# A Mamba scan on one core: the first convolution tap on GpSimd, the second batch's preparation two chunks sooner

## The chip, the core and the metric

The kernel runs on one core of a Trainium2 chip. The core has engines with a queue of instructions each: TensorE (PE: matmuls and transposes), VectorE (DVE), ScalarE (ACT), GpSimd (POOL) and SyncE (SP), which here only issues DMAs. A queue runs in the order in which it is written, and engines wait for one another on semaphores. The metric is the device time of one execution in microseconds (us); lower is better.

## The reference, cut to what matters

The reference takes x of shape (2, 1024, 128) through six layers: FFN, attention, FFN, mixture of experts (MoE), Mamba, MoE. Each stands behind a layer norm and is added back to x. The change lies in the Mamba layer, in float32, and where the MoE before it ends:

```python
x = x + 0.5 * _L1_ffn_ref(_layernorm(x, axis=-1), ...)        # MoE; "combining" adds its rows to x
x = x + _L1_attn_ref(_layernorm(x, axis=-1), ...)             # Mamba, forward and backward
# in one direction of Mamba:
zxbcdt = u @ Wi.T                                             # z, x|B|C (512 channels), dt
conv = conv_general_dilated(pad(xBC_t), conv_w, ...)          # 4 taps for each channel, along time
xBC = silu(conv + conv_b)
dt = softplus(dt + dt_bias);  A = -exp(A_log)                 # "step sizes"
h = h * exp(dt_t * A) + (dt_t * x_t) * B_t;  y_t = h @ C_t    # scan over 1024 steps
y = (y + D * x) * silu(z);  y = y * rsqrt(mean(y * y) + 1e-5) * norm_w;  out = y @ Wo.T
```

## The kernel before, in words

`moe_mamba_moe` (from L2363) writes the queues of all engines out by hand, for MoE, scan and MoE. The scan has four units, each one direction of one batch (units 0 and 1 are batch 0, units 2 and 3 are batch 1). A unit is worked off in 8 chunks of 128 time steps; `u` is the unit, `i` the chunk in it, and `g = 8 * u + i` counts chunks through. I write "chunk 1.2" for unit 1, i = 2. While unit u is scanned, the input of unit u + 1 is prepared, and these tables say in which chunk:

```python
PIECES_AT = [(0,), (1,), (2,), (3,), (), (4,), (5,), ()]
TAPS_AT = [((0, 1), (0, 2)), ((0, 3), (1, 1)), ((1, 2), (1, 3)), ((2, 1), (2, 2)), ((2, 3), (3, 1)), ((3, 2), (3, 3)), (), ()]
```

A unit's input has six pieces of 128 channels: pieces 0 to 3 are x|B|C and go through the convolution, 4 and 5 are z. PE projects a piece in two halves (L2083) into two PSUM banks that are used in turn, each taken again only when its last reader is through. ACT copies a half out to `mb_padded` (L2097), and then multiplies the whole row by the first tap into `mb_act` (L2110, `first_tap`). DVE adds taps 1 to 3 (L2119, `convolve`): the pair (c, k) in TAPS_AT is piece c, tap k. A tap 1 waits for the first tap of its piece. In chunk i = 6 ACT loads the Silu table, puts piece 4 and the four convolved pieces through Silu (L2097, L2126), and only then can PE transpose the next unit's first chunk.

In each chunk DVE does, in this order: `front(g + 1)` (`mb_xdt` L2184 and `mb_gm` L2188 from PSUM, then `mb_mt` L2191 from `mb_e_seg`, which ACT makes with an Exp, L2166), `pass_state(g)` (`mb_h` L2237 or L2234), `back(g)` (`mb_y_old` L2270, `mb_y_in` L2272 or L2274), the output additions of the unit before, the taps of TAPS_AT, and what else is put into the chunk. POOL does `mb_xw` of g + 1 (L2203), the gate of g (`mb_z`, L2281) and the decayed state for g + 1 (`mb_h_dec`, L2222). ACT's `exps(g + 1)` (L2159, L2164, L2166) needs `mb_cums`, which SP loads by a DMA, and PE's transposed B (L2145).

Batch 1's preparation is spread over these chunks: `combine` (L1823, L1825) and `stats_of` (L1110, L1116) add the MoE's rows to x and take means and variances; ACT takes the root (`norm.root`, a Sqrt table, L1121); DVE normalises (`norm.normalise`, L1150, L1156); PE transposes (`norm.turn`, L1164) and ACT copies out (`norm.copy`, L1171). Then PE's `steps` (L1940) gives the raw step sizes, DVE's `step_sizes` (part 0 at L2051 and L2053, parts 1 to 3 from L2056 to L2070) and ACT's `exp_dt` (L1963) turn them into dt and decays, and PE's `sums` with ACT's `exp_sums` into their running sums.

## Time and profile before

| | |
|---|---|
| median of 3 runs | 825.32 us (821.44 to 828.21) |
| the profiled execution, its own time | 819.01 us |
| its span in the trace | 817.2 us |
| scan (from the first `mb_xdt` to the last chunk) | about 471 to 673 us in the trace |
| busy share of the span | PE 88%, DVE 60%, ACT 66%, POOL 34% |

Times in rows are microseconds from the start of the span. The shares are means over stages that have different limits, so the stretch from 471 to 673 us has to be read by itself. A row of the timeline gives the start, the busy time, the engine, the line, the operation with output and inputs, and in square brackets how long the engine was idle before it and what ended that. Several equal instructions in sequence stand as one row with their count.

### The profile page before, as it was taken

Reading aid. Unit: us, or ns where it says so; the run is one execution under the profiler, and the core shown is the slowest. Engines: PE = TensorE matmul, PEld = TensorE weight load, DVE = VectorE, ACT = ScalarE, POOL = GpSimd, SP = SyncE. Lnnn points to the kernel's source line nnn. Section 1 sums busy time; section 2 is a strip of 40 time slices with the busy share of each in tenths; the row PEclk is TensorE's granted clock in tenths of the full one; section 3 lists DMA queues with packets and bytes.
Section 4 is the critical chain, followed back from the end, with each engine's and each line's share of the span. In section 5 each row is a group of like instructions: output and inputs, shape, how many; then the busy total and the mean of one; then the engine's idle time right before and its main releaser. Section 6 shows DMA issues by size and latency. Waiting matters only on the chain. (4 is left out here: it accounts for less than half of the span.)

```text
span 817.2 us, 13088 instructions
## 1 busy us (share of the span) xinstructions
PE 715.5 (88%) x4076; PEld 377.9 (46%) x4076; DVE 489.4 (60%) x1424; ACT 542.0 (66%) x934; POOL 275.2 (34%) x296
## 2 busy tenths in 40 slices
PE   4799999979999997988988867798888987999996
PEld 1432222212223223555655545576575775566564
DVE  6878442204766565763466649789697875533453
ACT  5367998888998993653357666885987642434441
POOL 3090003301000342435522445343443380265552
PEclk9899999999999997999999988899998898999999
DMA  4056934521493311112121031121211231222233
GB/s 136 1 203 165 186 86 88 207 76 53 138 317 85 110 37 40 44 34 62 42 80 46 26 109 60 52 65 53 74 60 50 81 84 39 65 61 57 67 99 92
DMA packets 76409, 70.10 MB, mean 86 GB/s; under 512 B 9687, under 2 KB 60233, under 8 KB 76080
## 3 DMA queue, kind: packets, MB, share of 16 engines
q1 hardware_dynamic: 71024, 60.56, 26.6%
q0 software_dynamic: 5024, 8.54, 3.2%
q8 instruction: 36, 0.59, 0.3%
q14 instruction: 37, 0.30, 0.1%
q10 hardware_dynamic: 288, 0.10, 0.0%
HBM read 41.23 MB, written 29.02 MB: 86 GB/s over the span
## 5 line engine op out<-in xcount | busy, mean ns | idle before, releaser
L693 ACT ACTIVATE attn_p<-attn_ps 128x1024 f32<-128x1024 f32 x256 | 241.1, 1083 | 28.5 <-PE attn_ps L686 17.2
L709 PE MATMUL attn_ps<-attn_p,attn_v 128*32 128x512 f32 x1024 | 138.1, 611 | 5.5 <-issue 5.5
L1687 PE MATMUL ps_main<-moe_xsT,moe_w 128*128 128x320 f32 x384 | 127.9, 459 | 8.5 <-DVE moe_hid L1712 3.3
L1697 ACT ACTIVATE moe_act_h<-ps_main 128x320 f32<-128x320 f32 (+1 forms) x128 | 55.2, 434 | 102.5 <-PE ps_main L1687 72.2
L1712 DVE TENSOR_TENSOR moe_hid<-moe_act_h,ps_main 128x320 f32<-128x320 f32 (+1 forms) x128 | 61.9, 485 | 91.1 <-ACT moe_act_h L1697 57.4
L1580 POOL DMA_INDIRECT moe_slots<-rows,moe_scatter_at x64 | 63.4, 991 | 103.0 <-DVE moe_hid L1712 53.8
L1687 PEld LDWEIGHTS ps_main<-moe_xsT,moe_w 128*128 128x128 f32 x384 | 68.8, 195 | 42.5 <-issue 21.8
L686 PE MATMUL attn_ps<-attn_q_rows,attn_k_rows 64*128 64x512 bf16 x448 | 80.6, 388 | 6.4 <-issue 3.1
L1717 PE MATMUL ps_main<-moe_hid,moe_w 128*128 128x320 f32 (+1 forms) x256 | 73.3, 451 | 4.6 <-DVE moe_hid L1712 4.6
L686 PEld LDWEIGHTS attn_ps<-attn_q_rows,attn_k_rows 64*128 64x128 bf16 x448 | 19.1, 93 | 124.0 <-ACT attn_p L693 99.0
L2119 DVE SCALAR_TENSOR_TENSOR mb_act<-mb_padded,mb_taps,mb_act 128x1024 f32<-128x1024 f32 x48 | 65.9, 1382 | 9.0 <-ACT mb_act L2110 8.3
L1717 PEld LDWEIGHTS ps_main<-moe_hid,moe_w 128*128 128x128 f32 (+1 forms) x256 | 41.1, 188 | 33.0 <-issue 13.1
L2281 POOL TENSOR_TENSOR mb_z<-mb_y_in,mb_z 128x256 f32<-128x256 f32 x24 | 26.4, 1098 | 49.8 <-DVE mb_y_in L2272 32.4
L1798 POOL DMA_INDIRECT moe_rows<-moe_y,moe_dest x33 | 31.9, 966 | 32.3 <-ACT moe_y L1789 13.6
L709 PEld LDWEIGHTS attn_ps<-attn_p,attn_v 128*32 128x32 f32 x1024 | 20.5, 108 | 47.1 <-issue 35.3
L1201 POOL TENSOR_TENSOR x_sb<-x_sb,bout_half 128x1024 f32<-128x1024 f32 (+1 forms) x4 | 7.3, 1822 | 103.5 <-DVE rows L1156 103.5
L2159 ACT ACTIVATE mb_e_seg<-mb_cums,mb_cum_col 128x128 f32<-128x128 f32 x128 | 40.5, 390 | 1.7 <-DMA mb_cums<-mb_cum_kept 1.7
L442 POOL TENSOR_SCALAR attn_parts<-attn_q 128x512 bf16<-128x512 f32 x4 | 2.5, 617 | 110.0 <-DVE attn_q L398 110.0
L2191 DVE TENSOR_TENSOR mb_mt<-mb_e_seg,mb_gm 128x512 f32<-128x512 f32 x32 | 26.4, 825 | 18.3 <-ACT mb_e_seg L2166 15.9
L2203 POOL TENSOR_TENSOR mb_xw<-mb_xdt,mb_to_end 128x256 f32<-128x256 f32 x28 | 18.5, 662 | 54.0 <-DVE mb_xdt L2184 54.0
L2083 PE MATMUL ps_side<-norm_xT,mb_w_xbc 128*128 128x512 f32 x64 | 31.8, 618 | 0.0
L727 DVE COPY attn_mixed<-attn_ps 128x512 f32<-128x512 f32 x10 | 6.9, 687 | 41.6 <-PE attn_ps L709 41.6
(268 smaller groups left out, 1304.5 us busy)
## 6 DMA issues: line engine op xcount, KB each, us to landing
mb_cums<-mb_cum_kept SPq DMA_DIRECT2D x32, 256.0 KB, 3.4
moe_slots<-zeros SPq DMA_DIRECT2D x4, 1380.0 KB, 13.4
attn_q_rows<-attn_q_parts SPq DMA_DIRECT2D x36, 128.0 KB
attn_k_rows<-attn_k_parts SPq DMA_DIRECT2D x36, 128.0 KB
moe_w<-in_w SPq DMA_DIRECT2D x3, 1536.0 KB, 11.6
moe_rows<-zeros SPq DMA_DIRECT2D x4, 1024.0 KB, 14.7
moe_back<-moe_rows SPq DMA_DIRECT2D x16, 256.0 KB, 3.8
mb_e_cum<-mb_e_cum_kept SPq DMA_DIRECT2D x56, 64.0 KB, 2.7
```

Of the source, the lines that this page charges most:

```text
L686: ins = self.core.nc.tensor.matmul(into, self.k_rows[rows, ring, pair, keys], self.q_rows[rows, ring, pair, queries], start=True, stop=True)
L693: self.core.nc.scalar.activation(self.p[:, w % self.PB, :, :].rearrange("p a n -> p (a n)"), self.ps_s[:, w % self.SB, :, :].rearrange("p ...
L709: ins = self.core.nc.tensor.matmul(self.ps_av[32 * i:32 * i + 32, :], self.v[:, b * TPB + kt, (HGROUPS * i + m) // 2, self.window(m)], sel ...
L1580: nc.gpsimd.indirect_dma_start(self.slots[r], bass.IndirectOffsetOnAxis(self.scatter_at[:, b, k, j:j + 1], 0), self.row_of[:, b * TPB + j, ...
L1687: self.core.nc.tensor.matmul(ps[:, w % 2, 0:CAP], wt[:, e, c * P:(c + 1) * P], self.xsT[:, u % 2, :], start=True, stop=True).then_inc(self ...
L1697: self.core.nc.scalar.activation(self.act_h[into, w % 2, :], self.ps_h1[rows, w % 2, 0:CAP], ACT.Silu).then_inc(self.silu_done, 1)
L1712: self.core.nc.vector.tensor_tensor(self.hid[rows, u % 2, c, :], self.act_h[rows, w % 2, :], bank[rows, w % 2, 0:CAP], ALU.mult)\
L1717: return self.core.nc.tensor.matmul(self.y_bank(u)[:, 0:CAP], self.w2[rows, u % E_, c, :], self.hid[rows, u % 2, c, :], start=start, stop= ...
L1798: self.core.nc.gpsimd.indirect_dma_start(self.rows[u // E_], bass.IndirectOffsetOnAxis(self.dest[0:n, u % self.DEST, s:s + 1], 0), self.y[ ...
L2083: self.core.nc.tensor.matmul(bank[:], weight, self.xT[:, t0:t0 + BANK], start=True, stop=True).then_inc(self.proj_done, 1)
L2119: ins = self.core.nc.vector.scalar_tensor_tensor(out, src, tap, out, ALU.mult, ALU.add)
L2159: ins = nc.scalar.activation(self.e_seg[:, g % 2, hh, :], self.cums[:, g % 2, hh, :], ACT.Relu, bias=self.cum[:, di, n, hh:hh + 1], scale= ...
```

## The change: what it does

- First taps move from ACT to POOL: `first_tap_beside` is a `tensor_scalar` of 128x1024 with (tap, 1.0). The first tap of piece 0 stands ahead of the gate in chunk i = 0; those of pieces 1, 2 and 3 stand at the end of POOL's chunks i = 1, 2, 3.
- Piece 0 of units 1, 2 and 3 is projected and copied out one chunk sooner: before the first chunk for unit 1, in chunk 0.7 for unit 2 and in chunk 1.7 for unit 3.
- Batch 1's combining and statistics move from chunks 0.3 and 0.4 to 0.1 and 0.2; roots from 0.6 to 0.4; normalising from 0.6 to 0.4; PE's turns from 0.7 to 0.5, and their copies with them.
- `steps` moves from chunk 1.1 to 0.7, `step_sizes` part 0 from 1.1 to 0.7, parts 1 to 3 from 1.2 to 1.0, `exp_dt` from 1.2 to 0.7, `sums` from 1.3 to 1.1 and `exp_sums` from 1.4 to 1.1.

On POOL, chunks 0.0 and 0.1, before (`mb_xw` L2203, the gate `mb_z` L2281, `mb_h_dec` L2222):

```order
L2203 TENSOR_TENSOR mb_xw<-mb_xdt,mb_to_end 128x256 x2
L2281 TENSOR_TENSOR mb_z<-mb_y_in,mb_z 128x2x128
L2222 TENSOR_TENSOR mb_h_dec<-mb_h,mb_whole 128x256
L2203 TENSOR_TENSOR mb_xw<-mb_xdt,mb_to_end 128x256
L2281 TENSOR_TENSOR mb_z<-mb_y_in,mb_z 128x2x128
L2222 TENSOR_TENSOR mb_h_dec<-mb_h,mb_whole 128x256
```

and with the change (the same lines stand seven further down):

```order
L2210 TENSOR_TENSOR mb_xw<-mb_xdt,mb_to_end 128x256 x2
L2117 TENSOR_SCALAR mb_act<-mb_padded,mb_taps 128x1024
L2288 TENSOR_TENSOR mb_z<-mb_y_in,mb_z 128x2x128
L2229 TENSOR_TENSOR mb_h_dec<-mb_h,mb_whole 128x256
L2210 TENSOR_TENSOR mb_xw<-mb_xdt,mb_to_end 128x256
L2288 TENSOR_TENSOR mb_z<-mb_y_in,mb_z 128x2x128
L2229 TENSOR_TENSOR mb_h_dec<-mb_h,mb_whole 128x256
L2117 TENSOR_SCALAR mb_act<-mb_padded,mb_taps 128x1024
```

The first tap of piece 1 (the second L2117) stands behind the gate and `mb_h_dec` of its chunk; the one of piece 0 stands ahead of the gate.

On DVE, from the taps of chunk 0.4 to the taps of chunk 0.5, with the change (before, L1823 to L1116 stood where L1150 and L1156 stand here, and the two pairs of L1150 and L1156 stood in chunk 0.6, behind the last taps):

```order
L2126 SCALAR_TENSOR_TENSOR mb_act<-mb_padded,mb_taps,mb_act 128x1024 x2
L1150 RECIPROCAL norm_rstd<-norm_std 128x4
L1156 TENSOR_SCALAR rows<-x_sb,norm_mv,norm_rstd 128x128 x4
L1150 RECIPROCAL norm_rstd<-norm_std 128x4
L1156 TENSOR_SCALAR rows<-x_sb,norm_mv,norm_rstd 128x128 x4
L2191 TENSOR_TENSOR mb_xdt<-ps_main,mb_dt 128x256
L2195 TENSOR_TENSOR mb_gm<-ps_main,mb_incl 128x128
L2198 TENSOR_TENSOR mb_mt<-mb_e_seg,mb_gm 128x512
L2244 TENSOR_TENSOR mb_h<-mb_h_dec,ps_main 128x256
L2277 TENSOR_TENSOR mb_y_old<-mb_e_cum,ps_main 128x256
L2279 TENSOR_TENSOR mb_y_in<-mb_y_old,ps_main 128x256
L2126 SCALAR_TENSOR_TENSOR mb_act<-mb_padded,mb_taps,mb_act 128x1024 x2
```

Normalising batch 1 now lies between the taps of two chunks, ahead of `mb_xdt` of chunk 0.6.

On ACT, from the four Silus of chunk 0.6 to the Exp for chunk 1.1, before:

```order
L2126 ACTIVATE mb_act<-mb_act,mb_conv_b 128x1024 x4
L2097 ACTIVATE mb_z<-ps_side 128x512 x2
L2290 ACTIVATE mb_y<-mb_z 128x256
L2159 ACTIVATE mb_e_seg<-mb_cums,mb_cum_col 128x128 x4
L2164 COPY mb_bs<-ps_main 128x128
L2166 ACT_TABLE_LOAD
L2166 ACTIVATE mb_e_seg<-mb_e_seg 128x512
L2290 ACTIVATE mb_y<-mb_z 128x256
L1171 COPY norm_xT<-ps_side 128x512 x2
L2159 ACTIVATE mb_e_seg<-mb_cums,mb_cum_col 128x128 x4
L2164 COPY mb_bs<-ps_main 128x128
L2166 ACTIVATE mb_e_seg<-mb_e_seg 128x512
```

and with the change:

```order
L2133 ACTIVATE mb_act<-mb_act,mb_conv_b 128x1024 x4
L2097 ACTIVATE mb_z<-ps_side 128x512 x2
L2297 ACTIVATE mb_y<-mb_z 128x256
L2166 ACTIVATE mb_e_seg<-mb_cums,mb_cum_col 128x128 x4
L2171 COPY mb_bs<-ps_main 128x128
L2173 ACT_TABLE_LOAD
L2173 ACTIVATE mb_e_seg<-mb_e_seg 128x512
L2297 ACTIVATE mb_y<-mb_z 128x256
L2097 ACTIVATE mb_padded<-ps_side 128x512 x2
L1963 ACTIVATE mb_ex<-mb_ab 128x64
L2166 ACTIVATE mb_e_seg<-mb_cums,mb_cum_col 128x128 x4
L2171 COPY mb_bs<-ps_main 128x128
L2173 ACTIVATE mb_e_seg<-mb_e_seg 128x512
```

The two copies of the normalised rows have left, and the two halves of piece 0 of unit 2 and the Exp of the step sizes (L1963) now stand ahead of `mb_e_seg` for chunk 1.1.

The diff:

```diff
--- before.py
+++ after.py
@@ -2109,6 +2109,13 @@
             act.wait_ge(self.y_read, self.NC * (u - 1))
         self.core.nc.scalar.activation(self.act_t[:, u % 2, c, :], src, ACT.Copy, scale=tap).then_inc(self.tapped, 1)
 
+    def first_tap_beside(self, pool, u, c):
+        src, tap = self.window(u, c, 0)
+        pool.wait_ge(self.proj_read, (u * self.PIECES + c) * 2 + 2)
+        if u >= 2:
+            pool.wait_ge(self.y_read, self.NC * (u - 1))
+        self.core.nc.gpsimd.tensor_scalar(self.act_t[:, u % 2, c, :], src, tap, 1.0, ALU.mult, ALU.mult).then_inc(self.tapped, 1)
+
     def convolve(self, dve, ch, u, c, k):
 
         (src, tap), out = self.window(u, c, k), self.act_t[:, u % 2, c, :]
@@ -2449,6 +2456,7 @@
                 pe.wait_ge(moe.y_read, 3 * HALF)
                 pe.wait_ge(mamba.norm_done, 2)
                 mamba.before(pe, 0)
+                mamba.project(pe, 1, 0)
                 for g in range(N):
                     u, i = g // NC, g % NC
                     if g + 1 < N:
@@ -2464,15 +2472,19 @@
                         mamba.output(pe, u, i - 6)
                     if u == 1 and i == 0:
                         pe.wait_ge(norm.ready, 20)
+                    if u == 0 and i == 5:
+                        norm.turn(pe, 18)
+                        norm.turn(pe, 19)
                     if u + 1 < UNITS:
                         for c in mamba.PIECES_AT[i]:
-                            mamba.project(pe, u + 1, c)
+                            if c:
+                                mamba.project(pe, u + 1, c)
+                    if u + 2 < UNITS and i == 7:
+                        mamba.project(pe, u + 2, 0)
                     if u == 0 and i == 7:
-                        norm.turn(pe, 18)
-                        norm.turn(pe, 19)
+                        pe.wait_ge(norm.ready, 20)
+                        mamba.steps(pe, 1)
                     if u == 1 and i == 1:
-                        mamba.steps(pe, 1)
-                    if u == 1 and i == 3:
                         mamba.sums(pe, 1)
                     if u == 2 and i == 7:
                         norm.turn(pe, 20)
@@ -2578,10 +2590,14 @@
                     u, i = g // NC, g % NC
                     if g + 1 < N:
                         mamba.to_state(pool, g + 1)
+                    if u < 3 and i == 0:
+                        mamba.first_tap_beside(pool, u + 1, 0)
                     if u < 3:
                         mamba.gate(pool, nc.gpsimd, g)
                     if i < NC - 1:
                         mamba.decay(pool, g + 1)
+                    if u < 3 and i in (1, 2, 3):
+                        mamba.first_tap_beside(pool, u + 1, i)
                     if u == 3 and 2 <= i <= 6:
                         moe.scatter(pool, 3, 3 * (i - 2), 3 * (i - 1) + (i == 6))
                 for u in range(HALF, 2 * HALF):
@@ -2674,15 +2690,15 @@
                     if u + 1 < UNITS:
                         for c, k in mamba.TAPS_AT[i]:
                             mamba.convolve(dve, ch, u + 1, c, k)
-                    if u == 0 and i in (3, 4):
-                        moe.combine(dve, ch, 1, i - 3)
-                        norm.stats_of(dve, ch, i + 15)
-                    if u == 0 and i == 6:
+                    if u == 0 and i in (1, 2):
+                        moe.combine(dve, ch, 1, i - 1)
+                        norm.stats_of(dve, ch, i + 17)
+                    if u == 0 and i == 4:
                         norm.normalise(dve, ch, 18)
                         norm.normalise(dve, ch, 19)
-                    if u == 1 and i == 1:
+                    if u == 0 and i == 7:
                         mamba.step_sizes(dve, ch, 1, 0)
-                    if u == 1 and i == 2:
+                    if u == 1 and i == 0:
                         for part in range(1, mamba.STEP_PARTS):
                             mamba.step_sizes(dve, ch, 1, part)
                     if u == 2 and i == 4:
@@ -2781,13 +2797,14 @@
                 moe.weigh(act, HALF - 1)
                 mamba.take(act, 0, 5)
                 mamba.exps(act, 0)
+                mamba.take(act, 1, 0)
                 for g in range(N):
                     u, i = g // NC, g % NC
                     if g + 1 < N:
                         mamba.exps(act, g + 1)
                     if g == 1:
                         act.wait_ge(moe.y_out[(HALF - 2) % moe.OUT], moe.landings(HALF - 2))
-                    if u == 0 and i == mamba.GATES_AT:
+                    if u == 0 and i == 4:
                         norm.root(act, 18)
                         norm.root(act, 19)
                     if u == 2 and i == mamba.GATES_AT:
@@ -2802,20 +2819,21 @@
                         mamba.deviation(act, 3)
                     if u + 1 < UNITS:
                         for c in mamba.PIECES_AT[i]:
-                            if c < 4:
+                            if 1 <= c < 4:
                                 mamba.take(act, u + 1, c)
-                                mamba.first_tap(act, u + 1, c)
                         if gates:
                             mamba.take(act, u + 1, 4)
                             mamba.silu_rows(act, u + 1)
                             mamba.take(act, u + 1, 5)
                             mamba.square(act, g - 1)
-                    if u == 0 and i == 7:
+                    if u == 0 and i == 5:
                         norm.copy(act, nc.scalar.copy, 18)
                         norm.copy(act, nc.scalar.copy, 19)
-                    if u == 1 and i == 2:
+                    if u + 2 < UNITS and i == 7:
+                        mamba.take(act, u + 2, 0)
+                    if u == 0 and i == 7:
                         mamba.exp_dt(act, 1)
-                    if u == 1 and i == 4:
+                    if u == 1 and i == 1:
                         mamba.exp_sums(act, 1)
                     if u == 2 and i == 7:
                         norm.copy(act, nc.scalar.copy, 20)
```

## Rows read from the trace of the kernel before

**Rows 1.** Busy time by stretch (header first): one inside unit 0, one inside unit 1.

```profile
core 0: us, PE busy (x) PEld busy (x) DVE busy (x) ACT busy (x) POOL busy (x), PEclk, DMA share, GB/s
...
487.00:521.00 34.00, 24.50 (x148) 17.94 (x149) 32.87 (x61) 21.94 (x51) 19.12 (x15) 0.90 0.20 64
...
537.00:575.00 38.00, 34.21 (x228) 26.00 (x225) 36.51 (x74) 27.21 (x65) 15.41 (x15) 0.96 0.19 55
```

**Rows 2.** DVE timeline: first taps 1 and 2 of units 1, 2, 3.

```profile
483.84 2.61 DVE L2119 SCALAR_TENSOR_TENSOR mb_act<-mb_padded,mb_taps,mb_act 128x1024 f32<-128x1024 f32 x2 [3.93 <-ACT mb_act L2110]
...
536.76 2.60 DVE L2119 SCALAR_TENSOR_TENSOR mb_act<-mb_padded,mb_taps,mb_act 128x1024 f32<-128x1024 f32 x2 [2.32 <-ACT mb_act L2110]
...
588.12 2.61 DVE L2119 SCALAR_TENSOR_TENSOR mb_act<-mb_padded,mb_taps,mb_act 128x1024 f32<-128x1024 f32 x2 [2.10 <-ACT mb_act L2110]
```

**Rows 3.** DVE timeline, units 0 and 1: the same operations alone and beside POOL.

```profile
476.69 0.69 DVE L2191 TENSOR_TENSOR mb_mt<-mb_e_seg,mb_gm 128x512 f32<-128x512 f32 x1 [0.63 <-ACT mb_e_seg L2166]
...
489.05 2.94 DVE L2119 SCALAR_TENSOR_TENSOR mb_act<-mb_padded,mb_taps,mb_act 128x1024 f32<-128x1024 f32 x2
...
492.63 0.95 DVE L2191 TENSOR_TENSOR mb_mt<-mb_e_seg,mb_gm 128x512 f32<-128x512 f32 x1
```

**Rows 4.** POOL timeline, chunk 0.1 and the start of 0.2.

```profile
489.21 1.70 POOL L2281 TENSOR_TENSOR mb_z<-mb_y_in,mb_z 128x256 f32<-128x256 f32 x1 [1.74 <-PE ps_main L2214]
490.88 1.59 POOL L2222 TENSOR_TENSOR mb_h_dec<-mb_h,mb_whole 128x256 f32<-128x256 f32 x1
492.43 0.61 POOL L2203 TENSOR_TENSOR mb_xw<-mb_xdt,mb_to_end 128x256 f32<-128x256 f32 x1
```

**Rows 5.** POOL timeline, attention stage: TENSOR_SCALAR with one tensor input, twice 512 columns.

```profile
52.36 1.20 POOL L450 TENSOR_SCALAR attn_parts<-attn_rest 128x512 bf16<-128x512 f32 x2
```

**Rows 6.** ACT timeline, unit 0: mb_e_seg of 0.2, the tables of 0.6, the copies of 0.7.

```profile
485.14 1.28 ACT L2159 ACTIVATE mb_e_seg<-mb_cums,mb_cum_col 128x128 f32<-128x128 f32 x4 [1.33 <-DMA mb_cums<-mb_cum_kept]
...
486.47 0.63 ACT L2166 ACTIVATE mb_e_seg<-mb_e_seg 128x512 f32<-128x512 f32 x1
...
517.04 1.28 ACT L1121 ACT_TABLE_LOAD   x1
...
518.84 1.28 ACT L2097 ACT_TABLE_LOAD   x1
...
530.13 1.07 ACT L1171 COPY norm_xT<-ps_side 128x512 f32<-128x512 f32 x2
```

**Rows 7.** DVE timeline, end of unit 0: mb_xdt of 0.6, normalising batch 1, mb_xdt of 1.0.

```profile
514.71 0.39 DVE L2184 TENSOR_TENSOR mb_xdt<-ps_main,mb_dt 128x256 f32<-128x256 f32 x1
...
522.69 0.17 DVE L1150 RECIPROCAL norm_rstd<-norm_std 128x4 f32<-128x4 f32 x1
...
524.55 1.11 DVE L1156 TENSOR_SCALAR rows<-x_sb,norm_mv,norm_rstd 128x128 f32<-128x128 f32 x4
526.56 0.42 DVE L2184 TENSOR_TENSOR mb_xdt<-ps_main,mb_dt 128x256 f32<-128x256 f32 x1 [0.91 <-PE ps_main L2142]
```

**Rows 8.** DVE timeline: mb_mt of 1.0 and 1.1, step-size part 0, mb_y_in of 2.0.

```profile
529.92 0.69 DVE L2191 TENSOR_TENSOR mb_mt<-mb_e_seg,mb_gm 128x512 f32<-128x512 f32 x1 [2.74 <-ACT mb_e_seg L2166]
...
533.08 0.69 DVE L2191 TENSOR_TENSOR mb_mt<-mb_e_seg,mb_gm 128x512 f32<-128x512 f32 x1 [1.15 <-ACT mb_e_seg L2166]
...
544.91 0.21 DVE L2051 TENSOR_TENSOR mb_v<-ps_side,mb_dt_bias 128x64 f32<-128x64 f32 x1
545.16 0.38 DVE L2053 SCALAR_TENSOR_TENSOR mb_ab<-mb_v 128x64 f32<-128x64 f32 x1
...
585.60 0.41 DVE L2274 COPY mb_y_in<-ps_main 128x256 f32<-128x256 f32 x1
```

**Rows 9.** PE timeline: one piece projected, the raw step sizes, and the turns.

```profile
529.46 1.07 PE L1164 MATMUL ps_side<-ident,rows 128*128 128x128 f32 x8
...
537.77 1.96 PE L2083 MATMUL ps_side<-norm_xT,mb_w_xbc 128*128 128x512 f32 x4
539.62 1.95 PE L1940 MATMUL ps_side<-mb_w_dt,norm_xT 128*128 128x8 f32 x16
```

## The prediction

> **What bounds the kernel now.** The change touches the scan alone, so I read the busy times of its stretches first, then each engine's timeline in it, to see what ends every wait. Inside a unit DVE is the bound: it is busy 32.87 of 34 us in chunks 0.1 to 0.5 and 36.51 of 38 us in unit 1, where ACT has 21.94 and 27.21 and POOL 19.12 and 15.41 [rows 1]. What adds time to DVE's queue there adds it to the kernel; what ACT is spared there gives nothing back. Only where units meet does DVE wait for others: 3.93, 2.32 and 2.10 us, 8.35 in all, for the first tap of piece 0 of units 1, 2 and 3 [rows 2], 0.91 us for the transposes behind ACT's Silus [rows 7], and 2.74 and 1.15 us for ACT's Exp [rows 8].
>
> The timelines of DVE and POOL have to be laid side by side, since they disturb each other. `mb_mt` takes 0.69 us alone and 0.95 us where POOL's `mb_xw` started 0.20 us before it [rows 3, 4]. A pair of taps takes 2.61 us alone and 2.94 us beside POOL [rows 2, 3]. The other way, of POOL's three operations on 256 columns `mb_xw` takes 0.61 us, but beside DVE's taps `mb_h_dec` takes 1.59 and the gate 1.70 us [rows 4]. The gate starts at 489.21, beside a tap that started at 489.05 and is 1.30 us long (half of 2.61), and ends at 490.91, some 0.55 us after that tap: it sat through the tap and then ran. The one that comes second waits for the other's whole instruction.
>
> **First tap of pieces 1: DVE waits for POOL, +6.3 us.** On POOL the tap of piece 1 stands behind the gate and `mb_h_dec` of chunk i = 1. DVE's second tap in that chunk is tap 1 of this very piece and needs it. The first tap on POOL costs 1.20 us by twice 512 columns of the same operation [rows 5]; ends are 0.61 us, what a 256-column operation takes [rows 4], and 2.4 us, twice the measured 1.20. I take 1.20, since the columns are the same and one tensor is read. From the row: the gate ends at 490.91, `mb_h_dec` would run alone now, as DVE stands still, 0.61 us, then the tap 1.20 us: 492.7. DVE's tap of 1.30 us ends at 494.05, where the pair now ends at 489.05 + 2.94 = 491.99 [rows 3]. So 2.1 us in each of three units. Behind the waiting tap on DVE's queue stands the whole next chunk, so nothing takes this up.
>
> **First taps of pieces 2 and 3: +5.0 us.** They stand at the end of POOL's chunks i = 2 and 3 and are needed a chunk later, so nobody waits for their result. But in unit 0 `mb_h_dec` ends at about 492.5, when DVE's taps are over and `mb_mt` is next [rows 3, 4]: the 1.20 us then lie before `mb_mt`, combining or the next unit's taps, all with two inputs in SBUF. A POOL operation of 0.61 us costs DVE 0.95 - 0.69 = 0.26, its length less 0.35. By that one of 1.20 costs 0.85, six times 5.0. The ends are 0.26 (1.6 in all) and the whole 1.20 (7.2). The Trainium skill, SBUF — State Buffer, "Who interferes with whom", has it that a DVE operation with two SBUF inputs and a GpSimd one that reads SBUF exclude each other for the whole instruction, and that whoever issues first has the pair; by its letter a tap costs DVE nothing or all of it. The same skill's Perfetto Trace Analysis, "Optimizing Scalar/DVE Operations", warns that work passed between these two engines may not help, which speaks against this change; the rows above agree.
>
> **First tap of piece 0 and the earlier copy.** This is the gain that the change can have, up to 8.35 us.
> - Unit 1: the taps can start at 479.9 instead of 483.84, but what follows them is `mb_mt` of chunk 0.2, and its `mb_cums` lands at 485.14, after which ACT needs till 487.10 [rows 6]. That DMA's place in SP's queue doesn't change. DVE waits there instead of ahead of the taps: gain 0.
> - Unit 3: `mb_y_in` of 2.0 ends at 586.01 and the taps start at 588.12, so 2.10 is to be had [rows 2, 8]. ACT now copies piece 0 ahead of its `mb_e_seg` for chunk 2.1, 1.07 us as for the two copies of the same width [rows 6], and POOL's tap falls beside that `mb_mt`, 0.5 us. I take -0.5, from -2.1 to +0.5.
> - Unit 2 has step sizes in its way, next.
>
> **Between units 0 and 1: +1.5 us.** The order on PE in 0.7 becomes: project piece 0 (1.96 us), `steps` (1.95 us) [rows 9], and then the transposes for 1.1, where before the 1.07 us of turns stood. `steps` takes the bank that ACT must first have copied out, behind the Exp of 1.0. With 529.46 for the start: projected 531.4, `steps` done 533.4, part 0 on DVE 0.6 us [rows 8] till 534.0, `exp_dt` on ACT till 534.3, and ACT's `exps` for 1.1, 1.96 us as from 485.14 to 487.10 [rows 6], till 536.2. `mb_mt` of 1.1 comes at 536.2 where it came at 533.08: +3.1. `mb_h` and `mb_y_in` follow, and the taps start at about 538.0, not 536.76: +1.2 although the tap wait of 2.32 is gone. Ahead of this, ACT is rid of the Sqrt table and roots in 0.6 (517.04 to 518.84, 1.8 us [rows 6]). But PE's turns now wait for DVE's normalising, which ends where `mb_xdt` of 0.6 starts, at 514.7 by the rows of before [rows 7]. The second turn takes half of 1.07, a copy on ACT half of 1.07, piece 4 in the freed banks 1.96 us behind them: 517.3; the transposes for 0.7 and ACT's last two steps of `exps` take 1.7 us more, an estimate, till 519.0, where that Exp now ends at 517.0. So ACT's way to the Silus is 2.0 us longer and 1.8 us shorter. Net about +0.3. The range of both is 0 to +3.5.
>
> **Batch 1's work.** Combining and statistics move between two chunks that are both full: 0. Normalising runs from 522.69 to 525.66 now, 3.0 us in the shadow of ACT's Silus, since DVE would wait till 526.56 anyway [rows 7]. In 0.4 it has no shadow and pushes everything behind it, ACT's Silus too, since these follow the transposes that follow DVE: **+3.0**. It would cost nothing only if ACT or PE were late in 0.5, and they aren't. `step_sizes` part 0 leaves a full chunk for the wait between units: -0.6 [rows 8]. Parts 1 to 3 go from one full chunk to another, 0. `sums` and `exp_sums` move on PE and ACT, which have room inside units [rows 1]. SP's queue is the same. Twelve first taps leave ACT: 0, where it has room.
>
> **Sum.** 6.3 + 5.0 + 0 - 0.5 + 1.5 + 3.0 - 0.6 = **+14.7 us**. On the profiled execution's own 819.0 us this is 833.7; that run lies 6.3 us under the median of 825.3. Against the median I forecast **840 us**. By the lower ends (waits for piece 1 at 1.5 each = 4.5, others 1.6, -2.1, 0, 3.0, -0.6) it is +6.4, 832; by the upper ones (waits at 3.3 = 9.9 with a 2.4 us tap, 7.2, +0.5, +3.5, +3.0, -0.6) +23.5, 849. The Trainium skill, GPSIMD Engine Reference, "Engine selection", sends elementwise work to VectorE and calls GpSimd with one input roughly line-rate; taking DVE's 1.30 us for the same columns as line-rate I would estimate a sum 0.9 us higher.
>
> **Rivals.** About 1%, 8.2 us, is the least that this kernel's measurement tells from no change.
> - *A wash.* Taps cost DVE what the short POOL operations cost, 0.26 each, and the gaps between units give back what the rows hold (2.10 at unit 3, all of the 2.32 at unit 2): 6.3 + 1.6 - 2.1 - 2.3 + 3.0 - 0.6 = +5.9, 831. For it: POOL idles half of each chunk [rows 1]. Against it: POOL's idle part lies before the gate, not behind it, and the step sizes stand in the way. Chance 0.20.
> - *Faster.* The three waits for piece 0 go for good (-8.35), the roots' 1.8 us leave the way to the Silus, and POOL's taps fit: 825.3 - 10.2 = 815. It turns on chunk i = 1: if POOL's tap of piece 1 ends before DVE's first tap of that chunk does (1.3 us behind `mb_y_in`), nobody waits. For it: 3.93 us is the longest of the waits. Against: gate and `mb_h_dec` stand ahead of it and are held up by that same DVE tap [rows 4]; normalising would have to be free too. Chance 0.08.
> - *Whole-instruction lock.* By the skill's rule above, where POOL always comes first: 7.2 instead of 5.0, and the same again for the taps of piece 0 beside `mb_mt` and for `mb_xw` queued behind a tap, 1.2 us three times: +20.5, 846. For it: POOL's queue is ready at the moment at which DVE ends its taps. Against: DVE's short PSUM operations lie between and take no harm. Chance 0.10.
> - Forecast: 0.62.
>
> The range 829 to 848 takes in the forecast with its bounds, the lock and half of the wash. Faster by over 1%: 0.08. Within 1% (817 to 833.5): the wash and a little of the forecast, 0.21. Slower: 0.71.
>
> **What would show it.** Right: in chunks 0.1, 1.1 and 2.1 a wait of about 2 us on DVE for POOL's L2117 ahead of a tap, and none in front of the first taps; the wait for `mb_e_seg` in front of `mb_mt` of 0.2 grown to over 3 us; `mb_mt` over 1.2 us long behind POOL's taps of pieces 2 and 3; L1156 ahead of `mb_xdt` of 0.6 and a wait of 3 to 4 us at the end of unit 0; `mb_mt` of 1.1 over 5 us behind that of 1.0. Wrong: POOL's L2117 under 0.8 us; no wait in i = 1; DVE idle in 0.4 to 0.6, which would make normalising free; or the step from 0.7 to 1.1 not longer than before.

## The result: slower by 1.5%, and the profile after

| | before | changed |
|---|---|---|
| median of the runs shown | 825.34 us (4 runs, 821.44 to 828.21) | 833.98 us (4 runs, 830.7 to 838.54) |
| ratio | 1 | 1.0153, 95% interval 1.0109 to 1.0197 |
| profiled execution, its span | 819.0, 817.2 us | 830.7, 828.8 us |

The forecast was 840 us, 829 to 848, slower with a chance of 0.71. Runs that the chip disturbed are left out of every ratio here, and e1 and e4 below, whose only traces came from such runs, are told without one.

The scan starts 0.3 us later than before, and its last `mb_xdt` comes 11.2 us later; the span grew by 11.6 us. So all of it is in the scan. In the tables and rows that follow, lines from L2112 on have moved by 7 (the taps are L2126, `mb_xdt` L2191, `mb_mt` L2198; the new tap is L2117). The control e9 and e12 have the numbers of before, e10 and e11 numbers 3 higher than the changed kernel's.

The table of waits of the changed kernel, VectorE from 465 to 690 us (total, times, longest), answers to the three waits for ScalarE's first tap in [rows 2]: these are gone, and three for GpSimd's stand there.

```profile
DVE mb_mt L2198 <- ACT mb_e_seg L2173: 19.5, 9, 3.2
DVE mb_xdt L2191 <- PE ps_main L2149: 13.6, 4, 7.0
DVE mb_act L2126 <- POOL mb_act L2117: 6.9, 3, 2.3
DVE mb_v L2051 <- PE ps_side L1940: 3.6, 1, 3.6
```

**Piece 0.** Rows of VectorE: the taps of unit 1 and the `mb_mt` of 0.2 behind them, and, in unit 3's preparation, the `mb_mt` of 2.1 beside GpSimd's tap of 594.05 to 595.17.

```profile
479.22 2.94 DVE L2126 SCALAR_TENSOR_TENSOR mb_act<-mb_padded,mb_taps,mb_act 128x1024 f32<-128x1024 f32 x2
...
484.92 0.69 DVE L2198 TENSOR_TENSOR mb_mt<-mb_e_seg,mb_gm 128x512 f32<-128x512 f32 x1 [2.23 <-ACT mb_e_seg L2173]
...
594.34 1.37 DVE L2198 TENSOR_TENSOR mb_mt<-mb_e_seg,mb_gm 128x512 f32<-128x512 f32 x1 [1.11 <-ACT mb_e_seg L2173]
```

**Piece 1.** Chunk 0.1 on VectorE (first fence) and GpSimd (second), timeline rows of the changed kernel: start, length, what is idle before it in brackets.

```profile
486.65 1.28 DVE L2126 SCALAR_TENSOR_TENSOR mb_act<-mb_padded,mb_taps,mb_act 128x1024 f32<-128x1024 f32 x1
490.22 1.28 DVE L2126 SCALAR_TENSOR_TENSOR mb_act<-mb_padded,mb_taps,mb_act 128x1024 f32<-128x1024 f32 x1 [2.29 <-POOL mb_act L2117]
```

```profile
486.81 1.71 POOL L2288 TENSOR_TENSOR mb_z<-mb_y_in,mb_z 128x256 f32<-128x256 f32 x1 [3.60 <-DVE mb_y_in L2279]
488.47 0.61 POOL L2229 TENSOR_TENSOR mb_h_dec<-mb_h,mb_whole 128x256 f32<-128x256 f32 x1
489.07 1.12 POOL L2117 TENSOR_SCALAR mb_act<-mb_padded,mb_taps 128x1024 f32<-128x1024 f32 x1
```

The pair of taps lasts from 486.65 to 491.50, 4.85 us, where it lasted 2.94 [rows 3]: 1.9 us. The gate is held up by VectorE's first tap, `mb_h_dec` then runs its 0.61 us alone, and the tap takes 1.12 us. Chunks 1.1 and 2.1 have the same wait of 2.29 us.

**Pieces 2 and 3.** In 0.3 GpSimd's tap starts 0.18 us ahead of `mb_mt`, which takes 1.47 us and not 0.94. In 1.3 VectorE comes first: GpSimd's tap starts beside the second tap of VectorE's pair (568.96 to 571.79) and takes 2.09 us; most of what is left of it then lies beside `mb_xdt` and `mb_gm`, which read PSUM and only one tensor in SBUF, and which take no longer for it, and `mb_mt` takes 0.89 (0.94 before). VectorE's rows first, GpSimd's second.

```profile
509.71 1.47 DVE L2198 TENSOR_TENSOR mb_mt<-mb_e_seg,mb_gm 128x512 f32<-128x512 f32 x1
...
568.96 2.83 DVE L2126 SCALAR_TENSOR_TENSOR mb_act<-mb_padded,mb_taps,mb_act 128x1024 f32<-128x1024 f32 x2
571.71 0.41 DVE L2191 TENSOR_TENSOR mb_xdt<-ps_main,mb_dt 128x256 f32<-128x256 f32 x1
...
572.42 0.89 DVE L2198 TENSOR_TENSOR mb_mt<-mb_e_seg,mb_gm 128x512 f32<-128x512 f32 x1
```

```profile
509.53 1.11 POOL L2117 TENSOR_SCALAR mb_act<-mb_padded,mb_taps 128x1024 f32<-128x1024 f32 x1
...
570.68 2.09 POOL L2117 TENSOR_SCALAR mb_act<-mb_padded,mb_taps 128x1024 f32<-128x1024 f32 x1
```

These rows give the price of standing beside one another. An operation of GpSimd and one of VectorE with two inputs in SBUF run one behind the other here: the later one ends at the end of the earlier one, plus its own length alone, less 0.15 us. `mb_mt` of 0.5 (0.69 us alone): 509.53 + 1.11 + 0.69 - 0.15 = 511.18, and it ends at 511.18. GpSimd's tap in 1.3: 571.79 + 1.12 - 0.15 = 572.76, and it ends at 572.77. `mb_mt` behind it: 572.77 + 0.69 - 0.15 = 573.31, as in the row. The 0.95 us of [rows 3] come out too, behind `mb_xw` [rows 4]: 493.04 + 0.54 = 493.58. So a tap on GpSimd costs VectorE what is left of it when VectorE wants to start, and nothing where VectorE's operation is first and done before the next such one.

**End of unit 0 and start of unit 1.** VectorE first, TensorE second. They answer to [rows 7 to 9].

```profile
515.28 1.20 DVE L1156 TENSOR_SCALAR rows<-x_sb,norm_mv,norm_rstd 128x128 f32<-128x128 f32 x4
...
517.64 0.42 DVE L2191 TENSOR_TENSOR mb_xdt<-ps_main,mb_dt 128x256 f32<-128x256 f32 x1
...
529.84 0.42 DVE L2191 TENSOR_TENSOR mb_xdt<-ps_main,mb_dt 128x256 f32<-128x256 f32 x1 [4.12 <-PE ps_main L2149]
...
533.65 0.69 DVE L2198 TENSOR_TENSOR mb_mt<-mb_e_seg,mb_gm 128x512 f32<-128x512 f32 x1 [3.18 <-ACT mb_e_seg L2173]
...
541.39 0.69 DVE L2198 TENSOR_TENSOR mb_mt<-mb_e_seg,mb_gm 128x512 f32<-128x512 f32 x1 [1.54 <-ACT mb_e_seg L2173]
...
542.66 2.94 DVE L2126 SCALAR_TENSOR_TENSOR mb_act<-mb_padded,mb_taps,mb_act 128x1024 f32<-128x1024 f32 x2
```

```profile
533.18 3.76 PE L2083 MATMUL ps_side<-norm_xT,mb_w_xbc 128*128 128x512 f32 x4
536.73 1.97 PE L1940 MATMUL ps_side<-mb_w_dt,norm_xT 128*128 128x8 f32 x16
```

Normalising now stands ahead of `mb_xdt` of 0.6 (515.09 to 517.64, 2.55 us), the stretch that it filled before is a wait of 4.12 us, and `mb_mt` of 1.1 comes 7.74 us behind that of 1.0, where it came 3.16 behind it. The projection that stands ahead of the raw step sizes takes 3.76 us for the same four matmuls that took 1.96 [rows 9]. The busy times by stretch (columns as in [rows 1]) say why: TensorE was granted 0.51 of its clock there, the lower of its two levels; a figure between 0.5 and 1 is a stretch that has both.

```profile
487.00:521.00 34.00, 27.15 (x122) 19.70 (x121) 30.80 (x63) 16.43 (x40) 18.93 (x16) 0.72 0.15 47
521.00:530.00 9.00, 6.01 (x40) 4.27 (x39) 4.70 (x9) 8.21 (x12) 3.47 (x3) 1.00 0.19 45
530.00:537.00 7.00, 7.00 (x27) 4.33 (x25) 1.91 (x5) 4.52 (x12) 1.34 (x2) 0.51 0.14 47
```

### The profile page after: what moved, and what is told of

Read it like the earlier page. It is cut to its first block and busy times, and to the rows that moved or that the text cites. A ratio compares the mean times of both kernels' runs of the same rounds, so it can differ in the third digit from the quotient of the medians.

```text
span 828.8 us, 13090 instructions
## 1 busy us (share of the span) xinstructions
PE 723.8 (87%) x4076; PEld 383.7 (46%) x4076; DVE 492.9 (59%) x1424; ACT 530.1 (64%) x923; POOL 295.4 (36%) x308
## 5 line engine op out<-in xcount | busy, mean ns | idle before, releaser
L709 PE MATMUL attn_ps<-attn_p,attn_v 128*32 128x512 f32 x1024 | 136.4, 604 | 5.7 <-issue 5.6
L1697 ACT ACTIVATE moe_act_h<-ps_main 128x320 f32<-128x320 f32 (+1 forms) x128 | 55.2, 434 | 102.9 <-PE ps_main L1687 73.1
L1580 POOL DMA_INDIRECT moe_slots<-rows,moe_scatter_at x64 | 63.8, 997 | 102.9 <-DVE moe_hid L1712 54.1
L2126 DVE SCALAR_TENSOR_TENSOR mb_act<-mb_padded,mb_taps,mb_act 128x1024 f32<-128x1024 f32 x48 | 67.1, 1403 | 7.5 <-POOL mb_act L2117 6.9
L2288 POOL TENSOR_TENSOR mb_z<-mb_y_in,mb_z 128x256 f32<-128x256 f32 x24 | 29.3, 1219 | 47.5 <-DVE mb_y_in L2279 41.7
L2198 DVE TENSOR_TENSOR mb_mt<-mb_e_seg,mb_gm 128x512 f32<-128x512 f32 x32 | 27.8, 867 | 21.9 <-ACT mb_e_seg L2173 19.5
L2221 PE MATMUL ps_main<-mb_xw,mb_bs 128*128 128x256 f32 x56 | 20.7, 455 | 16.4 <-DVE mb_h L2244 5.8
L2083 PE MATMUL ps_side<-norm_xT,mb_w_xbc 128*128 128x512 f32 x64 | 32.9, 636 | 0.0
```

What stands on the lines that cost most here:

```text
L709: ins = self.core.nc.tensor.matmul(self.ps_av[32 * i:32 * i + 32, :], self.v[:, b * TPB + kt, (HGROUPS * i + m) // 2, self.window(m)], sel ...
L1580: nc.gpsimd.indirect_dma_start(self.slots[r], bass.IndirectOffsetOnAxis(self.scatter_at[:, b, k, j:j + 1], 0), self.row_of[:, b * TPB + j, ...
L1697: self.core.nc.scalar.activation(self.act_h[into, w % 2, :], self.ps_h1[rows, w % 2, 0:CAP], ACT.Silu).then_inc(self.silu_done, 1)
L2083: self.core.nc.tensor.matmul(bank[:], weight, self.xT[:, t0:t0 + BANK], start=True, stop=True).then_inc(self.proj_done, 1)
L2126: ins = self.core.nc.vector.scalar_tensor_tensor(out, src, tap, out, ALU.mult, ALU.add)
```

## Experiments: one part taken back

The theory was the sum of terms: each part taken out of the changed kernel should give its term back. All ratios here and below are to runs of the kernel before on the same chip at the same time; here the kernel before had 828.29 us.

**e1_taps_on_act**: the first taps return to ScalarE.

```diff
-                    if u < 3 and i == 0:
-                        mamba.first_tap_beside(pool, u + 1, 0)
...
-                    if u < 3 and i in (1, 2, 3):
-                        mamba.first_tap_beside(pool, u + 1, i)
...
                                 mamba.take(act, u + 1, c)
+                            if c < 4:
+                                mamba.first_tap(act, u + 1, c)
```

> The changed kernel with all twelve first taps back on ACT (piece 0's in chunk i = 0, pieces 1 to 3 behind their copies); piece 0 still copied early, batch 1's work still early. Theory (first taps on POOL cost DVE a wait of 2.3 us in i = 1, three times, and port time in i = 2 and 3, together about 9 us against 5.9 saved nowhere): no DVE wait on a first tap of piece 1, and 834 - 9 = 825 us, level with the kernel before. Rival (the cost sits in batch 1's work, moved out of the shadow of ACT's Silus and into the step between units 0 and 1): the taps' place matters little since POOL idles anyway, and this stays at 832 to 835 us.

Measured: 837.72 us, ratio 1.0099 (1.0053 to 1.0144).

**e2_taps_ahead_of_gate**: GpSimd's taps of pieces 1 to 3 stand ahead of the gate of their chunk instead of behind the decay.

```diff
+                    if u < 3 and i in (1, 2, 3):
+                        mamba.first_tap_beside(pool, u + 1, i)
                     if u < 3:
                         mamba.gate(pool, nc.gpsimd, g)
                     if i < NC - 1:
                         mamba.decay(pool, g + 1)
-                    if u < 3 and i in (1, 2, 3):
-                        mamba.first_tap_beside(pool, u + 1, i)
```

> The changed kernel with the first taps of pieces 1, 2 and 3 put ahead of the gate in POOL's chunks i = 1, 2, 3; they stay on POOL. Theory (what costs is POOL's order: gate and mb_h_dec ahead of the tap): the three waits of 2.29 us on DVE for POOL's L2117 are gone or under 0.5 us, the port time stays or grows a little, 834 - 5 = 829 us. Rival (what costs is that two engines share a read port, wherever the tap stands): the time stays within 2 us of 834, the waits turning into longer mb_mt and longer tap pairs.

Measured: 840.17 us, ratio 1.0134 (1.0063 to 1.0205).

**e3_batch1_as_before**: batch 1's combining, normalising, turning and step sizes stand where they stood before; GpSimd keeps the taps, and pieces 0 of units 1 and 3 stay early.

```diff
-                    if u == 0 and i in (1, 2):
-                        moe.combine(dve, ch, 1, i - 1)
-                        norm.stats_of(dve, ch, i + 17)
-                    if u == 0 and i == 4:
+                    if u == 0 and i in (3, 4):
+                        moe.combine(dve, ch, 1, i - 3)
+                        norm.stats_of(dve, ch, i + 15)
+                    if u == 0 and i == 6:
                         norm.normalise(dve, ch, 18)
...
-                    if u == 0 and i == 7:
+                    if u == 1 and i == 1:
                         mamba.step_sizes(dve, ch, 1, 0)
```

> The changed kernel with all of batch 1's work (combining, roots, normalising, turns, step sizes, sums) and piece 0 of unit 2 back in their old chunks; first taps stay on POOL, piece 0 of units 1 and 3 stays early. Theory (normalising in 0.4 costs DVE 2.55 us, and the longer way from 0.7 to 1.1 costs 4.6 less the 2.3 of the tap wait): about 5 us less, 829 us; the wait ahead of mb_xdt of 1.0 is down from 4.12 to 1 us. Rival (batch 1's work only changes place between full chunks and the taps on POOL cost everything): 834, no less than 832 us.

Measured: 843.45 us, ratio 1.0183 (1.0112 to 1.0255).

**e4_steps_as_before**: only the step sizes of batch 1 (the second hunk above, with the matmuls and exponentials that belong to it) go back.

> The changed kernel with only the step sizes of batch 1 (steps, step_sizes, exp_dt, sums, exp_sums) back in chunks 1.1 to 1.4; normalising stays in 0.4 and unit 2's piece 0 stays early. Theory (steps in 0.7 stands between the transposes of 1.0 and 1.1 on PE and so holds up mb_mt of 1.1, 4.6 us later against mb_mt of 1.0 than before): mb_mt of 1.1 comes some 4 us behind mb_mt of 1.0 and not 7.7, part 0 costs 0.6 in 1.1: 834 - 3 = 831 us. Rival (the piece's projection at 1.2 GHz, 3.76 us, is what holds it up): mb_mt of 1.1 stays over 6 us behind that of 1.0 and the time at 833 to 834.

Measured: 839.85 us, ratio 1.0132 (1.0097 to 1.0167).

None of the four hit the theory's number: as ratios these were 1.000, 1.004, 1.004 and 1.007, each outside its interval. e1, e2 and e4 are as slow as their rivals had it, e3 at least so. But the rivals contradict one another: that of e1 puts the price in batch 1's work, that of e3 in the taps. So subtraction alone decides neither.

Read in the traces, e2 did what it was to do: the pair of taps in 0.1 takes 3.47 us and VectorE waits for no tap on GpSimd anywhere.

```profile
490.55 3.47 DVE L2126 SCALAR_TENSOR_TENSOR mb_act<-mb_padded,mb_taps,mb_act 128x1024 f32<-128x1024 f32 x2
```

From the first `mb_xdt` of unit 0 to that of unit 3 it needs 165.7 us where the changed kernel needs 169.0. But from there to the last chunk it needs 38.5 us and not 33.6, in a stretch that the edit doesn't touch. The busy times of that stretch, of e2 and then of the changed kernel, in both from about the `mb_xdt` of 3.3 on:

```profile
658.00:668.00 10.00, 10.00 (x64) 9.19 (x64) 6.28 (x17) 5.16 (x14) 5.39 (x7) 0.67 0.32 94
```

```profile
658.00:668.00 10.00, 9.21 (x80) 8.28 (x80) 9.48 (x27) 8.01 (x21) 7.26 (x9) 1.00 0.40 112
```

TensorE is busy the whole 10 us at 0.67 of its clock, and VectorE, which was the bound, is busy 6.28 of 10 us. In e3 the same happens ahead of chunk 2.1: VectorE waits 2.36 us for transposes behind a projection of 3.76 us. Its two stretches there:

```profile
585.00:590.00 5.00, 3.20 (x23) 2.64 (x23) 1.17 (x4) 4.98 (x11) 1.34 (x2) 0.81 0.01 2
590.00:595.00 5.00, 5.00 (x13) 2.83 (x13) 1.44 (x3) 2.81 (x6) 0.72 (x1) 0.51 0.29 66
```

So there is a price that belongs to no term: where the lower level falls. Whether the part that was taken out moves it, or it falls elsewhere from one execution to the next, one trace of each kernel can't tell; the two traces of the kernel before (the second is e9, below) show that it does the latter. It was no use to go on by subtraction.

## Experiments: one part added to the kernel before

The other way round, each part alone on the kernel before, with the kernel before itself once more as one of the four. The kernel before had 830.84 us here.

**e5_early_pieces_alone**: only the first pieces are projected and copied out sooner (unit 1's ahead of the scan, unit 3's at the end of unit 1; unit 2's stays, since the step sizes that made room for it do).

```diff
                 mamba.before(pe, 0)
+                mamba.project(pe, 1, 0)
...
                         for c in mamba.PIECES_AT[i]:
-                            mamba.project(pe, u + 1, c)
+                            if c or u == 1:
+                                mamba.project(pe, u + 1, c)
+                    if u == 1 and i == 7:
+                        mamba.project(pe, u + 2, 0)
```

> Only the first pieces of units 1 to 3 are projected and copied out a chunk sooner; batch 1 and the first taps stay as they were. The four kernels that each took one part of the change back (taps on ScalarE 1.010 of before, taps ahead of the gate 1.013, batch 1 as before 1.018, step sizes as before 1.013) all kept this part and none came back to before's time. Theory (the terms of the traces): the early pieces are worth about -0.5 us at each of two boundaries and nothing ahead of unit 1, so the ratio to before is 0.998 to 1.001, about 0 to -1 us. Rival (the part that all four share is the dear one, through TensorE's granted clock at the unit boundaries): 1.007 to 1.012, +6 to +10 us, with projection matmuls at 1.2 GHz in the chunk after each boundary.

Measured: 828.62 us, ratio 0.9989 (0.9948 to 1.0030). The theory's number; the rival falls. In its trace VectorE waits 2.35 us for transposes behind a projection of 3.76 us ahead of 2.1, as in e3: the rival's mechanism is there, in an execution that took 5.7 us more than the median, and not its price.

**e7_taps_on_pool_alone**: the four first taps go to GpSimd at the places of the change, and nothing else.

```diff
                                 mamba.take(act, u + 1, c)
-                                mamba.first_tap(act, u + 1, c)
...
+                    if u < 3 and i == 0:
+                        mamba.first_tap_beside(pool, u + 1, 0)
                     if u < 3:
                         mamba.gate(pool, nc.gpsimd, g)
                     if i < NC - 1:
                         mamba.decay(pool, g + 1)
+                    if u < 3 and i in (1, 2, 3):
+                        mamba.first_tap_beside(pool, u + 1, i)
```

> The kernel before with nothing changed but that the first tap of pieces 0 to 3 goes from ScalarE to GpSimd, at the places that the change gives them. Theory: three waits of VectorE of about 1.9 us on the tap of piece 1 (5.7 us), 2.7 us of VectorE made slow beside the taps of pieces 2 and 3 and 1 us beside that of piece 0: +8 to +10 us, ratio 1.010 to 1.012. Rival (taps are cheap, the price is elsewhere, since taking them back gave only 0.5%): +2 to +5 us, 1.003 to 1.006.

Measured: 841.84 us, ratio 1.0132 (1.0069 to 1.0195), +11 us. The interval takes in the theory's range and leaves out the rival's. Without the early copies VectorE waits for GpSimd six times, 15.6 us in all, three times for piece 0. The three waits for piece 1 are again 2.29 us.

**e8_batch1_alone**: the other half of the diff, batch 1's work two chunks sooner.

```diff
+                    if u == 0 and i == 5:
+                        norm.turn(pe, 18)
+                        norm.turn(pe, 19)
...
+                        pe.wait_ge(norm.ready, 20)
+                        mamba.steps(pe, 1)
                     if u == 1 and i == 1:
-                        mamba.steps(pe, 1)
-                    if u == 1 and i == 3:
                         mamba.sums(pe, 1)
```

> The kernel before with nothing changed but batch 1: combined and measured in chunks 1 and 2 of unit 0, normalised in chunk 4, turned in chunk 5, step sizes in chunk 7 and in chunk 0 of unit 1. Theory: 2.5 us from the normalising, which leaves the stretch in which VectorE waited, and 2 to 3 us for the step sizes' wait between chunks 0 and 1 of unit 1: +4 to +6 us, ratio 1.005 to 1.007. Rival (batch 1 is free, since the kernel with batch 1 as before was no faster than the changed one): 0.998 to 1.002.

Measured: 837.46 us, ratio 1.0076 (1.0034 to 1.0118), +6.3 us: just over the theory's range, which the interval takes in; the rival's 1.000 lies outside.

**e9_before_again**: the kernel before, unchanged.

> The kernel before, unchanged, as one more kernel of this call: what two identical kernels differ by here, and a second trace of it. Both theories: ratio 1.000 within 0.004; the start of the scan within 8 us of the first trace's 471.4 us, which shows how much of that start differs between executions of one kernel.

Measured: 828.72 us, ratio 0.9993 (0.9952 to 1.0035); its scan starts at 474.5 us, 3.1 us later than in the first trace of the same kernel. It is the control below.

The three parts add up to -0.1 + 1.3 + 0.8 = 2.0%, against the 1.5% of all together (1.1 to 2.0): within the intervals the parts add. The earlier copy of piece 0 of unit 2, which needs both the first and the third part, is in none of them.

## Experiments: which tap, which move, and taps nobody waits for

The kernel before had 822.0 us here.

**e10_piece1_on_pool**: e7 for piece 1 alone, with a semaphore of its own for GpSimd's taps.

```diff
+            if u and c in (1,):
+                dve.wait_ge(self.tapped_beside, 1 * (u - 1) + (1,).index(c) + 1)
...
+                    if u < 3 and i in (1,):
+                        mamba.first_tap_beside(pool, u + 1, i)
...
-                                mamba.first_tap(act, u + 1, c)
+                                if c not in (1,):
+                                    mamba.first_tap(act, u + 1, c)
```

> The kernel before, but the first tap of piece 1 alone goes to GpSimd, behind the gate and the decay of chunk 1. Theory (the wait is the price): in each of three units VectorE waits 2.3 us for the tap in chunk 1, of which 1.9 us are new: +5.7 us, ratio 1.007. Rival (the price of the taps is what they take from VectorE beside them, or an effect of GpSimd that grows with every tap there): a quarter to a third of the +11 us that all four taps cost, 1.003.

Measured: 830.73 us, ratio 1.0105 (1.0054 to 1.0156), +8.6 us. The waits are there (2.29, 2.29, 2.28 us), the theory's 1.007 lies in the interval and the rival's 1.003 does not. The trace shows where more than 5.7 us come from. TensorE turns batch 1's rows at the start of unit 1. The busy times ahead of that and around it, control first, e10 second:

```profile
522.00:528.00 6.00, 5.17 (x16) 2.59 (x16) 5.34 (x17) 6.00 (x9) 1.20 (x2) 0.66 0.11 35
528.00:534.00 6.00, 5.89 (x52) 4.95 (x51) 2.38 (x7) 5.97 (x17) 1.47 (x3) 1.00 0.15 48
```

```profile
524.00:530.50 6.50, 2.89 (x12) 1.58 (x13) 5.84 (x18) 6.49 (x10) 1.70 (x2) 1.00 0.13 49
530.50:536.50 6.00, 6.00 (x33) 5.45 (x33) 1.89 (x6) 5.33 (x14) 1.34 (x2) 0.51 0.14 48
```

and the turns themselves on TensorE's timeline, control first:

```profile
529.73 1.07 PE L1164 MATMUL ps_side<-ident,rows 128*128 128x128 f32 x8
```

```profile
533.63 1.95 PE L1164 MATMUL ps_side<-ident,rows 128*128 128x128 f32 x8
```

In the control TensorE spends its time at the lower level ahead of the boundary, while VectorE is busy 5.34 of 6 us; behind the boundary, where VectorE waits for it, it has the full clock. In e10 it is the other way round, and VectorE waits 3.31 us for the first tap of piece 0 of unit 2 (1.14 in the control). From `mb_xdt` of 1.0 to these taps it is 12.47 us in e10 and 9.43 in the control. But the first trace of the same kernel has 10.20 us and a wait of 2.32 [rows 2], also with the lower level in it:

```profile
525.70:529.40 3.70, 3.70 (x25) 3.31 (x24) 0.62 (x2) 3.67 (x10) 0.61 (x1) 0.63 0.10 29
```

(The control had 1.00 from 527.0 to 529.7.) So part of what e10 has there comes and goes between executions of one kernel, and how much of it is the tap's doing isn't shown.

**e11_pieces23_on_pool**: the same for pieces 2 and 3 (`(1,)` is `(2, 3)` in the edit above). No tap on GpSimd is waited for.

> The kernel before, but the first taps of pieces 2 and 3 alone go to GpSimd; no instruction of VectorE waits for them. Theory: 0.5 to 0.8 us of VectorE's work beside each tap of piece 2 and 0 to 0.8 us beside that of piece 3: +2.7 us, ratio 1.003. Rival (working beside GpSimd is as dear as waiting for it): +5 to +6 us, 1.006 to 1.007.

Measured: 827.42 us, ratio 1.0083 (1.0049 to 1.0117), +6.8 us (4.0 to 9.6). The theory's 1.003 falls. The direct price is in the trace as expected, in unit 0 these two rows (0.96 and 0.69 us in the control):

```profile
500.21 1.48 DVE L2201 TENSOR_TENSOR mb_mt<-mb_e_seg,mb_gm 128x512 f32<-128x512 f32 x1
...
506.72 1.49 DVE L1825 TENSOR_TENSOR x_sb<-x_sb,moe_back 128x512 f32<-128x512 f32 x1
```

That is 1.3 us in unit 0 and 0.6 us in each of units 1 and 2, 2.5 in all. The rest is waits at the boundaries: 1.73 us for the transposes of 1.0 (0.45 in the control), 2.32 and 3.74 for the first taps of piece 0 of units 2 and 3 (1.14 and 2.10), 4.1 us together more than in the control. The two waits for taps go with TensorE's clock again; that of 1.73 was not followed back. The projections of unit 2's and unit 3's first pieces ran at the full clock, but the short matmuls ahead of them did not (0.57 from 530.0 to 534.0); around 2.1, e11 first and the control second:

```profile
585.50:591.50 6.00, 6.00 (x33) 4.87 (x32) 3.00 (x7) 5.08 (x13) 1.76 (x2) 0.50 0.16 53
```

```profile
579.00:585.50 6.50, 5.30 (x48) 4.60 (x48) 2.36 (x7) 6.47 (x18) 0.83 (x2) 1.00 0.12 42
```

From `mb_xdt` of 2.0 to the taps e11 needs 11.51 us and the control 9.42. That the taps on GpSimd put the lower level there isn't shown: at 1.0 the first trace of the kernel before has it too, and there the first taps of unit 2 are waited for 2.32 us as in e11.

**e12_norm_sooner**: batch 1 is combined, normalised and turned two chunks sooner; the step sizes stay.

```diff
-                    if u == 0 and i in (3, 4):
-                        moe.combine(dve, ch, 1, i - 3)
-                        norm.stats_of(dve, ch, i + 15)
-                    if u == 0 and i == 6:
+                    if u == 0 and i in (1, 2):
+                        moe.combine(dve, ch, 1, i - 1)
+                        norm.stats_of(dve, ch, i + 17)
+                    if u == 0 and i == 4:
                         norm.normalise(dve, ch, 18)
```

> The kernel before, but batch 1 is combined in chunks 1 and 2, normalised in chunk 4 and turned in chunk 5 of unit 0; its step sizes stay in chunks 1 and 2 of unit 1. Theory: the normalising leaves the stretch ahead of unit 1 in which VectorE waited: +2.5 us, 1.003, and the other 3.8 us of batch 1's +6.3 us belong to the step sizes. Rival: all of it is here, 1.007, or none, 1.000.

Measured: 828.85 us, ratio 1.0092 (1.0052 to 1.0132), +7.6 us. The rival (all of batch 1's price is here) holds, and with e8 at 1.0076 the times give the move of the step sizes no price (-1.3 us, some 5 either way). The trace of e8 does: from `mb_xdt` of 1.0 to the taps it has 14.95 us where e12 and the control have 9.43, and the raw step sizes ran at the lower level, 3.56 us for the 1.95 of [rows 9]. That execution took 7 us more than e8's median, so the two don't contradict each other, and the price of this move stays open.

```profile
542.27 3.56 PE L1940 MATMUL ps_side<-mb_w_dt,norm_xT 128*128 128x8 f32 x16
```

ScalarE's and VectorE's rows at the end of unit 0, of e12 (first and second) and of the control (third):

```profile
529.22 0.27 ACT L2164 COPY mb_bs<-ps_main 128x128 f32<-128x128 f32 x1 [2.54 <-PE ps_main L2145]
...
532.30 4.26 ACT L2126 ACTIVATE mb_act<-mb_act,mb_conv_b 128x1024 f32<-128x1024 f32 x4
```

```profile
537.31 0.42 DVE L2184 TENSOR_TENSOR mb_xdt<-ps_main,mb_dt 128x256 f32<-128x256 f32 x1 [5.29 <-PE ps_main L2142]
```

```profile
522.77 4.26 ACT L2126 ACTIVATE mb_act<-mb_act,mb_conv_b 128x1024 f32<-128x1024 f32 x4
```

From the start of the scan, ScalarE's Silus begin at 54.1 us in e12 and at 48.2 in the control, 5.9 later (49.7 in the first trace of the kernel before). Of that 1.3 us arise up to `mb_xdt` of 0.2, ahead of all that the edit moves, and less than two executions of the kernel before differ by there (13.31 and 14.92 us); 2.4 us from there to `mb_xdt` of 0.7 are the normalising; and 2.3 us lie in front of ScalarE's copy: TensorE turns batch 1 (2.35 us) and projects a `z` piece (3.62 us, clock 0.50) ahead of the transposes for which ScalarE waits 2.54 us. Out of its shadow the work is paid for on VectorE, and a second time in ScalarE's chain behind the turns where TensorE has its lower level: the changed kernel's `z` projection took 2.49 us at that place.

**e13_early_pool_0_3**: e5 with the first taps of pieces 0 and 3 on GpSimd, those that VectorE didn't wait for in the changed kernel (`(0, 3)` in the edit of e10).

> The kernel with early pieces alone (0.999 of before), and GpSimd takes the first taps of pieces 0 and 3, for which VectorE never waited in the changed kernel. Theory (a tap on GpSimd costs only by a wait or by what runs beside it): +0.3 us beside each tap of piece 0 and 0 to 0.6 us beside piece 3, less nothing, since ScalarE's 2.3 us per unit are not waited for: 1.000 to 1.002 of before. Rival (ScalarE's load is waited for at the unit boundaries): 0.993 to 0.997, faster than both kernels. Rival (any tap on GpSimd costs as much as that of piece 1): 1.005 or more.

Measured: 823.16 us, ratio 1.0016 (0.9983 to 1.0048). The theory's number, with both rivals' outside the interval, the second just so: six taps moved for nothing gained or lost, with one wait of 1.2 us for them. No version here is faster than the kernel before.

The time from the first `mb_xdt` of each unit to the next one's (of unit 3 to its last chunk), in us, one trace each; how much longer the traced execution took than the median of its kernel; and the median granted clock of the runs:

| | unit 0 | unit 1 | unit 2 | unit 3 | ratio | traced less median | clock |
|---|---|---|---|---|---|---|---|
| before, first trace | 55.1 | 52.1 | 50.6 | 33.8 | 1 | -6.3 | 0.952, 0.955 |
| control e9 | 53.2 | 52.1 | 50.6 | 35.2 | 0.9993 | -1.3 | 0.957 |
| e5, early pieces | 53.8 | 54.4 | 53.0 | 35.2 | 0.9989 | +5.7 | 0.954 |
| e13 | 53.1 | 52.0 | 50.4 | 33.9 | 1.0016 | -3.7 | 0.957 |
| e10, piece 1 | 54.9 | 57.2 | 52.6 | 36.1 | 1.0105 | +3.1 | 0.950 |
| e11, pieces 2 and 3 | 55.7 | 53.5 | 53.3 | 33.9 | 1.0083 | +0.4 | 0.947 |
| e12, normalising | 59.1 | 52.2 | 50.6 | 33.9 | 1.0092 | +1.3 | 0.947 |
| e7, all taps | 57.0 | 55.2 | 56.3 | 34.9 | 1.0132 | +6.9 | 0.950 |
| e8, batch 1 | 57.3 | 59.4 | 51.1 | 35.2 | 1.0076 | +7.1 | 0.954 |
| changed | 58.1 | 57.6 | 53.4 | 33.6 | 1.0153 | -3.3 | 0.949 |

(The kernel before had 0.952 beside e5 to e9 and 0.955 beside e10 to e13.) One trace is one execution: e5, which costs nothing by its runs, has a scan of 196.4 us in its trace, as long as that of e11, and 5 us longer than the control's. So the table shows where time can go, and the ratios what a change costs.

## Why the prediction was right, and where its sum was off

- **Sign, size and range** held: 834 us measured, +1.5% where +1.8% was forecast, and the waits and slowed operations that it named stand in the trace. That the size came so near is in part luck: two terms were too large as direct costs, and the lower level of TensorE's clock, which the sum didn't have, came on top. Put together as the traces have them, with -2.2 us in unit 1's preparation for a term that was taken as 0, the terms are 5.7 + 2.7 - 2.2 - 0.2 + 3.0 + 2.6 - 0.6 = 11.0 us; from the first to the last `mb_xdt` the scan grew by 10.9. That it is so close is chance as well, since shifts of under 1 us are left out.
- **First tap of piece 1, +6.3 us.** Right. Each wait costs 1.9 us and not 2.1, 5.7 us in all, mostly because the tap takes 1.12 us and not 1.20. Alone (e10) it costs 8.6 us (4.4 to 12.8); the point of the *faster* rival (the tap ends before VectorE's first tap does) is missed by 2.29 us every time.
- **First taps of pieces 2 and 3, +5.0 us.** As a direct cost too large: 0.8 + 0.53 us in unit 0, 0.73 + 0 and 0.62 + 0 in units 1 and 2, 2.7 us. Where the tap met two-input operations of VectorE it cost 0.53 to 0.80, near the 0.85 that was worked out (0.53 is 0.78 less the 0.26 that `mb_xw` no longer takes from that `mb_mt`). That in units 1 and 2 piece 3's would start behind a tap of VectorE and then lie beside PSUM operations was not seen. Alone (e11) they cost 6.8 us, so as a net price 5.0 was the better number, for a reason that the sum did not hold. The whole-instruction lock was given a chance of 0.10 as a rival; as a mechanism it is borne out. The rows above end as if each later operation waited for the whole earlier one, which is also the prediction's own reading that whoever comes second waits. The rival's price failed because GpSimd isn't always first, and where it is, part of its operation is over when VectorE's starts. Here the Trainium skill (SBUF — State Buffer, "Who interferes with whom") has an exclusive lock between a VectorE operation with two SBUF inputs and a GpSimd one that reads SBUF, and the rows agree; "for the whole instruction" it says of VectorE's two-port modes. Its clause that a VectorE operation with at most one SBUF input does not contend agrees with `mb_xdt` in 1.3, 0.41 us beside the tap and 0.41 or 0.42 elsewhere.
- **First tap of piece 0.** Right as a net, as far as runs can tell: e5 gives 0.9989, some 3.4 us either way, where 0 and -0.5 us were taken. At unit 3 the wait of 2.10 is gone, but `mb_mt` of 2.1 takes 1.37 us for 0.69 beside the tap, and from the first `mb_xdt` of unit 2 to its third it takes 11.75 us for 11.94: -0.2. In the changed kernel the taps of unit 1 did start sooner (479.22 for 483.84), and `mb_mt` of 0.2 came 2.2 us sooner too, not at the same time: its `mb_cums` landed earlier. Counted from the first `mb_mt` it comes after 9.79 us, in the kernel before after 12.29 and, in the control's execution of the same kernel, 11.05; so 1.2 us of it come without any change, and the rest stays open. The wait of over 3 us in front of it was 2.23 here, 3.66 in e2.
- **Between units 0 and 1, +1.5 us.** Mis-sized in this trace: +3.0 from `mb_xdt` of 0.6 to the taps. Up to `mb_xdt` of 1.0 it is +0.35 (12.20 us for 11.85), for the +0.3 that stood against each other there; from there it is +2.6 for +1.2. The step that failed is "projected 531.4", 1.96 us for a projection that took 3.76 at the lower level of TensorE's clock. As a price of moving the step sizes the times neither bear out nor exclude 1.5: e8 less e12 is -1.3 us and the changed kernel less e4 +1.7 us, each with an error of some 5 us. Part 0 of the step sizes, -0.6 in the sum, took 0.56 us in 1.1 before and stands in the wait between the units now.
- **Normalising, +3.0 us.** Right as a direct cost: 2.55 us on VectorE, and the shadow that it left is the wait of 4.12 us. As the net price of the move it was too small: e12 puts 7.6 us (4.3 to 10.9) on it. Of the turns ahead of ScalarE's Silus, which the sum had at +0.3, it shows 2.3 us (13.69 for 11.40 from `mb_xdt` of 0.6 to that of 1.0), because of the clock.
- **What the sum left out altogether** is TensorE's clock. Durations on TensorE were taken from rows at full clock, and where the stretches at the lower level lie differs from kernel to kernel and between the two traces of the kernel before. Its clock in the runs goes with the time: of the runs of the kernel before beside the last four kernels the one at 0.943 took 827.6 us, the one at 0.967 took 816.0. Among kernels it goes with the time less well: five that cost time have 0.947 to 0.950, those that don't 0.952 to 0.957, and e8 with 0.954 costs time all the same. Whether the lower clock is cause or follower of the waits, these runs can't part.

## What to carry to other kernels

An operation passed to an idle engine is paid for by who waits for it: put at the end of that engine's queue it cost 1.9 us each time although the engine idled half of every chunk, while the taps of pieces 0 and 3, for which hardly anyone waited, cost nothing (e13). That nobody waits is not enough, though: nobody waited for the taps of pieces 2 and 3 in e11 either, and it cost 6.8 us, 2.5 of them because GpSimd's operation was first at the SBUF data that VectorE's next one wanted. Work that stands in a wait is free; moved "sooner" into a full stretch it costs its whole length, and everything that follows it on the other engines too. To find what the parts of a change cost, add each alone to the kernel before: taken back one at a time from the changed kernel, they gave back less than they cost, and one trace of each could not say why. Trace the old kernel twice before a difference of a few us in a trace is put down to the change.

## What the hardware showed

- The same four projection matmuls (L2083) took 1.96 us at granted clock 1.00 and 3.76 us at 0.51. The lower level came behind stretches in which TensorE had idled: busy 2.89 of 6.50 us ahead of it in e10, 3.20 of 5.00 in e3 (at a clock of 0.81, so part of it at the lower level already). But the changed kernel was busy 3.29 of 5.00 us at the same place and kept 1.00. So by these stretches how busy it had been just before doesn't decide it alone. TensorE: Matmul & The Clock Gate of the Trainium skill, "What's actually happening", has two levels only, set by recent business; the rows agree with the levels.
- A GpSimd operation of one SBUF input on 1024 columns took 1.11 or 1.12 us where VectorE was still or came later, and 1.54 to 2.09 behind a VectorE operation with two SBUF inputs. It and such operations of VectorE ran one behind the other: the later one ended 0.15 us sooner than the sum of the earlier one's end and its own length alone (`mb_mt` at 511.18 and 573.31, the tap at 572.77). The cost for VectorE's was 0.5 to 0.8 us.
- Two executions of one kernel differ by 3.1 us in when the scan starts, by 1.9 us in unit 0 and by 1.2 us in one wait (2.32 and 1.14) that goes with TensorE's clock. Medians of identical kernels differ by 0.07%, with an interval of 0.4% either way: terms under 3 us are not told apart here by times, and by traces only where the clock is the same.
